# Outputs as 2x2 and 4x2 pixel patches in a lattice of convolutions on one Trainium2 core

## The chip, the cores and the metric

The kernel runs on one core of a Trainium2 chip. The metric is the device time of one execution in microseconds.

## The reference, cut to what matters

The input x is 8 images of 16 channels of 64x64, fp32. Four blocks add to it in turn, each on a group-normalised copy:

```python
x = x + L0(gn(x))     # lattice: 4x4 cells, each a 3x3 convolution + bias + relu
x = x + L1(gn(x))     # 3x3 convolution, 16 to 16 channels, circular borders
x = x + L2(gn(x))     # KAN: 3x3 over silu(v) and 8 cubic B-splines of v (9 features)
x = x + L3(gn(x))     # 3x3 convolution with bias
```

A lattice cell takes one to three groups of 16 channels (from the left, from below, from above) and gives groups to the right, up and down. Only the last cell's right output is used, so cells need one to three outputs. A cell's kind is (inputs)(outputs): cell 0 is 12, 1 and 2 are 13, 3 is 12, 4, 7, 8 and 11 are 22, 5, 6, 9 and 10 are 33, 12 and 15 are 21, 13 and 14 are 31. `gn` takes mean and variance over pairs of channels of an image.

## The kernel before, in words

**Products.** Every convolution is done as matmuls of 512 columns in float32r, three products for each term: high part of the weights by high part of the data, high by low, low by high. `split_hi` (ACT, line 994) copies an input piece as its high part, `split_lo` (DVE, line 1197) subtracts to get the low part, and in some kinds a DVE copy (line 1203) lays a shifted or doubled version on partitions 64 to 127, so that two products share a matmul.

**Patches.** An output tile has row parity on its partitions: 16 channels x outputs x 2, 4 or 8 image rows. Columns are on the free axis, rows of 66 with a zero column on each side, so the three column shifts are three matmuls (`TERMS`, line 126).

**Lattice.** `STEPS` is 16 cells x 8 images; step s is one image of one cell. For each step SyncE (line 605) loads the inputs from `DIN` in HBM into one of `SLOTS_K` = 2 raw slots once the low parts of step s - 2 are done; ACT and DVE split into `SLOTS_F` = 3 pieces; TensorE (line 1441) runs the matmuls into a ring of four banks; ACT (line 1004) evacuates with bias and relu into one of `SLOTS_S` = 3 staging slots; POOL (line 726) stores each output group to the `DIN` of the cell that takes it, with one DMA per group. The load of step s waits for the stores of the same image one cell earlier. `input_loads` (line 177) gives one DMA per input group and one to four for its halo rows: 15 DMAs in a 33 cell, 10 in 22, 9 in 31, 6 in 21, 5 in 13 and 12. The rows outermost are 16 to 128 on both sides.

**Weights.** TensorE turns the taps of cell k + 2 during cell k (`turn`), POOL stores them (line 696) and spreads them into the banded matrix of the next cell, a few DMAs per step (line 704). KAN weights are summed on POOL in cell 5 and spread in cell 15.

**Stages after the lattice.** Circular convolution, KAN and last convolution run one after the other, eight images each (`block_step`, line 1466, and the KAN loop behind it). The halo rows of a tile are fetched from partition to partition by SyncE (`halo_block`, line 610, for the single convolutions; `feature_halo`, line 639, for KAN with two DMAs for each of nine features, i.e. 18 per image). In KAN, TensorE does 81 matmuls on an image's own features and then 27 on its halo rows; SyncE starts an image's halos only when the halo pass of the image before is over, as the halo tiles are single. Features (`basis_act`, and the DVE loop of `ROUNDS`) are made in two rounds per image:

```python
if b:
    sp.wait_ge(tile_used, used(b - 1, "halo"))
for g in range(KAN_SETS):
    sp.wait_ge(feat_lo, KAN_SETS * b + g + 1)
    for t in range(GROUP * g, GROUP * (g + 1)):
        feature_halo(t, halo_rows[g])
```

**Start.** SyncE and POOL load x with 64 DMAs of 32 KB; ACT's queue first brings eight small loads (two of them the single-row `OB_IN`) and then zeroes the border rows of all `DIN` tensors with 32 DMAs, taken as 16 channels x images x rows of 66 numbers.

Of the kernel before, what the change touches and what calls it, by code (L numbers as in the profile page):

```python
# [8 lines left out]
YI = 8  # L27
YB = 8
WD = 64
HT = 64  # L30
PW = WD + 2
PIX = YB * WD
B = 8
X_SPLIT = 5
OUT_SPLIT = 5
RING = 4
HALO = 2 * C
# [5 lines left out]
MAIN_TILES = NG * K3 * NG  # L43
TILES = MAIN_TILES + K3 * NG
FSLOTS = 8
# [3 lines left out]

CB_COLUMNS = 48  # L50
HALO_FEATS = 3
GROUP = 4
KAN_SETS = 2
ROUNDS = KAN_SETS * B

CHUNK = YB * PW
SLAB = CHUNK + 2 * PW
PIECE = 4 * CHUNK
KSLOT = 8 * CHUNK
# [3 lines left out]
SLOTS_O = 4  # L63

RIGHT, UP, DOWN = range(3)
GN_EPS = 1e-5


class Count:


    def __init__(self):
        self.base, self.n = 0, 0

    def next(self):
        self.n += 1
        return self.base + self.n

    def enter(self, base):
        self.base, self.n = base, 0  # L80


class Cell:


    def __init__(self, k, n_in, outs):
        self.k, self.n_in, self.outs = k, n_in, outs
        self.m = m = len(outs)
        self.ry = {3: 2, 2: 4, 1: 8}[m]
        self.nb = HT // self.ry  # L90
        self.rows = m * self.ry * C
        self.plane_rows = self.ry * C
        self.nq = YI // self.ry
        self.run = self.nb * PW
        self.chunks = self.nb // YB
        self.kind = f"{n_in}{m}"
        self.pieces = 2 if self.kind == "33" else 1
        self.in_rows = 6 * C if self.kind == "12" else P
        self.dup_at = {"33": 2 * CHUNK, "13": 0, "22": 2 * CHUNK, "21": 2 * CHUNK}.get(self.kind)


def lattice():

    cells = []
    for col in range(4):
        for row in range(4):
# [9 lines left out]
            if row < 3:  # L116
# [4 lines left out]

TERMS = {"33": [(0, 0, 0), (0, 1, 1), (0, 2, 2), (2 * CHUNK, 0, 3), (2 * CHUNK, 2, 4)],
         "13": [(0, 0, 0), (0, 2, 1)],
         "12": [(0, 0, 0), (0, 1, 1), (0, 2, 2)],
         "22": [(0, 0, 0), (0, 1, 1), (0, 2, 2), (2 * CHUNK, 0, 3), (2 * CHUNK, 2, 4)],
         "21": [(g * CHUNK, dx, g * K3 + dx) for g in range(2) for dx in range(K3)]
               + [(2 * CHUNK, 0, 6), (2 * CHUNK, 2, 7)],
         "31": [(g * CHUNK, dx, g * K3 + dx) for g in range(3) for dx in range(K3)]
               + [(3 * CHUNK, dx, 9 + dx) for dx in range(K3)]}
TILES_OF = {"33": 5, "13": 2, "12": 3, "22": 5, "21": 8, "31": 12}  # L130
SPLIT = {"33": 4 * CHUNK, "13": 4 * CHUNK, "12": 2 * CHUNK, "22": 4 * CHUNK, "21": 3 * CHUNK, "31": 4 * CHUNK}


W_AT = {5: 0, 9: 0, 6: 960, 10: 960, 0: 1920, 3: 1920, 1: 2688, 2: 3072,
        4: 3456, 8: 3456, 7: 4736, 11: 4736, 13: 6016, 14: 0, 12: 9216, 15: 9216}
WA_SIZE = 9216 + 2 * 8 * P
Z_AT, Z_SIZE = 6016, 3072


def kernel_rows(cell):  # L140

    ry = cell.ry
    k16 = C
    for g in range(cell.n_in):
        if cell.kind == "33" and g < 2 or cell.kind == "12":
            for r in range(ry):
                yield g, r, g * 4 * k16 + r * k16, 3, 0, 0, 3, 0
        elif cell.kind in ("33", "13"):
            tile = 3 if cell.kind == "33" else 0
            for r in range(ry):  # L150
                yield g, r, r * k16, 3, 0, 0, 1, tile
                yield g, r, 4 * k16 + r * k16, 3, 0, 1, 1, tile
                yield g, r, r * k16, 3, 0, 2, 1, tile + 1
        else:
            base, tile = (g * 4 * k16, 0) if cell.kind == "22" else (0, g * K3)
            for r in range(ry):
                first, last = max(r - 1, 0), min(r + 1, ry - 1)
                yield g, r, base + first * k16, last - first + 1, first - r + 1, 0, 3, tile
            for side, r, ky in ((0, 0, 0), (1, ry - 1, 2)):
                row = g * 2 * k16 + side * k16  # L160
                if cell.kind == "31":
                    yield g, r, row, 1, ky, 0, 3, 9
                else:
                    tile_b = 3 if cell.kind == "22" else 6
                    yield g, r, row, 1, ky, 0, 1, tile_b
                    yield g, r, 4 * k16 + row, 1, ky, 1, 1, tile_b
                    yield g, r, row, 1, ky, 2, 1, tile_b + 1


def banded_rows():  # L170

    for r in range(YI):
        first, last = max(r - 1, 0), min(r + 1, YI - 1)
        yield r, first * C, last - first + 1, first - r + 1


def input_loads(cell):

    ry, nq = cell.ry, cell.nq

    def halos(g, top, bottom, col):
        if nq > 1:
            yield top, C, col + CHUNK, nq - 1, g, ry - 1, 0, 0
        yield top, C, col, 1, g, YI - 1, 0, -1
        if nq > 1:
            yield bottom, C, col, nq - 1, g, 0, 1, 0
        yield bottom, C, col + (nq - 1) * CHUNK, 1, g, 0, 0, 1

    if cell.kind in ("33", "13", "12"):
        for g in range(cell.n_in):  # L190
            row, col = (0, cell.run) if g == 2 else (g * 4 * C, 0)
            yield row + C, ry * C, col, nq, g, 0, 0, 0
            yield from halos(g, row, row + C + ry * C, col)
    else:
        own = 1 if cell.kind == "22" else cell.n_in
        for g in range(cell.n_in):
            if cell.kind == "22":
                yield g * 4 * C, ry * C, 0, nq, g, 0, 0, 0
            else:
                yield 0, P, g * CHUNK, 1, g, 0, 0, 0  # L200
        for g in range(cell.n_in):
            yield from halos(g, g * 2 * C, g * 2 * C + C, own * cell.run)


def build(nc, x, l0w, l0b, l1w, l2base, l2spline, l2scale, l2bias, l3w, l3bias, consts, out):
# [7 lines left out]
    pieces_before, chunks_before = [0], [0]  # L213
    stores_before = [1]
    loads_before = [[0], [0]]
    loads_of = []
    for cell in cells:
        loads_of.append(len(list(input_loads(cell))))
        n_stores = sum(1 for _, to, _ in cell.outs if to is not None)
        stores_before.append(stores_before[-1] + n_stores)  # L220
# [3 lines left out]
    for s in range(STEPS):  # L224
        loads_before[s % SLOTS_K].append(loads_before[s % SLOTS_K][-1] + loads_of[s // B])
    TOTP, TOTCH = pieces_before[-1], chunks_before[-1]
    dups_before = [0]
    for cell in cells:
        for b in range(B * cell.pieces):
            dups_before.append(dups_before[-1] + (cell.dup_at is not None))  # L230
# [1349 lines left out]
```

## Time and profile before

| | us |
|---|---|
| median of 3 runs (lowest, highest) | 1571.28 (1570.34, 1573.9) |
| profiled execution, own time | 1571.25 |
| its span, first to last instruction | 1569.4 |
| PE busy | 1408.7 |
| DVE, ACT, POOL busy | 818.7, 733.4, 706.0 |

Busy times of different engines overlap. PE's time is that of matmuls, which are pipelined. A window row gives what each engine was busy within a stretch of the span, the mean granted TensorE clock as a share of 2.4 GHz, and the mean share of time that the 16 DMA engines were busy. The stretches used are the stages: 0 to 62.4 us is before the first lattice matmul, 62.4 to 262.6 cells 0 to 3, to 329.3 cell 4, to 562.6 cells 5 and 6, to 687.2 cells 7 and 8, to 920.6 cells 9 and 10, to 980.5 cell 11, to 1030.3 cell 12, to 1172.1 cells 13 and 14, to 1299.0 cell 15, the circular convolution and the filling of the first features, to 1515.7 KAN, and the rest the last convolution.

### The profile page before, as it was taken

Reading aid. Unit: us, or ns where it says so; the run is one execution under the profiler, and the core shown is the slowest. Engines: PE = TensorE matmul, PEld = TensorE weight load, DVE = VectorE, ACT = ScalarE, POOL = GpSimd, SP = SyncE. Lnnn points to the kernel's source line nnn. Section 1 sums busy time; section 2 is a strip of 40 time slices with the busy share of each in tenths; the row PEclk is TensorE's granted clock in tenths of the full one; section 3 lists DMA queues with packets and bytes.
Section 4 is the critical chain, followed back from the end, with each engine's and each line's share of the span. In section 5 each row is a group of like instructions: output and inputs, shape, how many; then the busy total and the mean of one; then the engine's idle time right before and its main releaser. Section 6 shows DMA issues by size and latency. Waiting matters only on the chain.

```text
span 1569.4 us, 17219 instructions
## 1 busy us (share of the span) xinstructions
PE 1408.7 (90%) x6048; PEld 1038.1 (66%) x6048; DVE 818.7 (52%) x704; ACT 733.4 (47%) x745; POOL 706.0 (45%) x1132
## 2 busy tenths in 40 slices
PE   0498898989999999989999999999999538999997
PEld 0365566756666677766666677777777427777775
DVE  5346643545545535545555444423237479898832
ACT  0356654434444444444444434332233569788621
POOL 4344687745743445422323458965646510121212
PEclk9999999999999999999999999999999778999988
DMA  6577778797777677798777767665544202222123
GB/s 120 145 194 192 191 199 212 188 197 173 181 185 156 148 181 188 192 180 181 180 163 168 170 155 186 173 186 141 157 123 108 48 8 42 41 36 43 31 42 52
DMA packets 153530, 221.85 MB, mean 141 GB/s; under 512 B 64612, under 2 KB 77252, under 8 KB 153444
## 3 DMA queue, kind: packets, MB, share of 16 engines
q1 hardware_dynamic: 97472, 134.53, 37.7%
q0 software_dynamic: 46208, 83.65, 20.3%
q10 hardware_dynamic: 9764, 2.57, 1.1%
q8 instruction: 48, 0.79, 0.2%
q14 instruction: 38, 0.31, 0.1%
HBM read 130.52 MB, written 79.46 MB: 134 GB/s over the span
## 4 chain that ended last, share of the span: by engine, by line
PE 73%; DVE 9%; POOL 4%; issue 3%; ACT 3%; DMA 3%; SPq 2%; ACTq 2%; DVEq 0%; POOLq 0%
PE PB L1441 60%; PE PB L1414 11%; POOL WA L712 2%; DMA S<-lattice_in 2%; DVE S L1326 2%; DVE F L1197 2%; SPq L605 1%; ACT F L994 1%; PE PB L1398 1%; DVE F L1203 1%; ACTq L1015 1%; POOL WA L704 1%; DVE F L1308 1%; ACTq L1014 1%; SPq L624 1%
## 5 line engine op out<-in xcount | busy, mean ns | idle before, releaser
L1441 PE MATMUL PB<-F,WA 128*96 128x512 f32 (+2 forms) x4512 | 1099.3, 405 | 52.7 <-DVE F L1203 21.5
L1441 PEld LDWEIGHTS PB<-F,WA 128*96 128x96 f32 (+2 forms) x4512 | 792.0, 176 | 350.4 <-issue 56.0
L1197 DVE TENSOR_TENSOR F<-S,F 128x2112 fp32r<-128x2112 f32 (+2 forms) x160 | 352.3, 2202 | 561.2 <-ACT F L994 561.1
L1004 ACT ACTIVATE S<-PB,BIAS 96x512 f32<-96x512 f32 (+1 forms) x320 | 218.9, 686 | 607.8 <-PE PB L1441 607.7
L726 POOL DMA_DIRECT2D lattice_in<-S x264 | 155.7, 595 | 523.9 <-ACT S L1004 509.8
L704 POOL DMA_DIRECT2D WA<-taps_cell x512 | 310.6, 614 | 10.6 <-issue 5.9
L994 ACT ACTIVATE F<-S 128x2112 fp32r<-128x2112 f32 (+2 forms) x160 | 292.0, 1825 | 39.5 <-DMA S<-lattice_in 39.3
L1414 PE MATMUL PB<-F,WA 128*128 128x512 f32 (+1 forms) x864 | 210.7, 404 | 33.7 <-DVE F L1308 33.7
L1414 PEld LDWEIGHTS PB<-F,WA 128*128 128x128 f32 (+1 forms) x864 | 163.1, 190 | 78.1 <-issue 35.8
L1203 DVE CAST F<-F 64x2110 fp32r<-64x2110 f32 (+2 forms) x128 | 172.0, 1344 | 4.5
L685 POOL TENSOR_TENSOR RS<-VE,NHALF 128x1 f32<-128x1 f32 (+1 forms) x25 | 30.9, 1235 | 260.5 <-DVE VE L1163 260.4
L1414 PE MATMUL PB<-F,W 128*128 128x512 f32 (+1 forms) x240 | 69.0, 442 | 12.3 <-DVE F L1243 11.1
L1414 PEld LDWEIGHTS PB<-F,W 128*128 128x128 f32 (+1 forms) x240 | 48.0, 208 | 30.2 <-issue 16.6
L696 POOL DMA_DIRECT2D taps_cell<-WT x68 | 39.3, 588 | 16.1 <-DVE WT L1110 15.8
L938 ACT ACTIVATE S<-S 128x2112 f32<-128x2112 f32 x16 | 31.5, 1968 | 22.4 <-DVE S L1317 22.4
L908 ACT ACTIVATE S<-KS,CB 128x528 f32<-128x528 f32 x64 | 41.8, 724 | 0.3
L1110 DVE TENSOR_TENSOR WT<-PB,WT 48x432 fp32r<-48x432 f32 (+6 forms) x19 | 8.7, 455 | 59.1 <-ACT WT L978 59.1
L1319 DVE TENSOR_TENSOR S<-S 128x2112 f32<-128x2112 f32 x16 | 37.6, 2352 | 2.5 <-ACT S L918 2.5
L1308 DVE TENSOR_TENSOR F<-S,F 128x2112 fp32r<-128x2112 f32 x16 | 37.6, 2352 | 2.0 <-ACT F L927 2.0
L1326 DVE SCALAR_TENSOR_TENSOR S<-S 128x2112 f32<-128x2112 f32 x16 | 37.7, 2357 | 0.0
L1339 DVE TENSOR_TENSOR S<-S 128x2112 f32<-128x2112 f32 x16 | 37.6, 2351 | 0.0
L712 POOL DMA_DIRECT2D WA<-taps_kan x52 | 33.4, 649 | 5.3 <-issue 5.3
(106 smaller groups left out, 531.9 us busy)
## 6 DMA issues: line engine op xcount, KB each, us to landing
S<-lattice_in SPq DMA_DIRECT2D x272, 264.0 KB, 3.9
lattice_in<-S POOLq DMA_DIRECT2D x264, 264.0 KB, 4.3
S<-lattice_in SPq DMA_DIRECT2D x704, 33.0 KB, 3.6
S<-lattice_in SPq DMA_DIRECT2D x224, 99.0 KB, 4.7
F<-F SPq DMA_DIRECT2D x144, 57.8 KB, 2.2
WA<-taps_cell POOLq DMA_DIRECT2D x192, 9.0 KB, 3.3
lattice_in<-KS POOLq DMA_DIRECT2D x8, 264.0 KB, 3.4
S<-S SPq DMA_DIRECT2D x48, 32.9 KB, 2.0
```

The costliest lines, as they stand in the source:

```text
L704: pool.dma_start(dst, src).then_inc(w_loaded[k % 2], 16)
L712: pool.dma_start(dst, src).then_inc(loaded, 16)
L726: pool.dma_start(dst, src).then_inc(image_stored[b], 16)
L908: last = act.activation(UA[n % 2][:, j * TS:(j + 1) * TS], NS[b % 2], ACT.Abs, scale=2.5, bias=CB[:, t:t + 1])
L994: act.activation(piece_view(s, h, 0), raw_view(s)[h], ACT.Copy).then_inc(hi_ready, 1)
L1004: act.activation(to[:, c * YB:(c + 1) * YB, 1:WD + 1], RING_BANK[n % SLOTS_O][0:cell.rows, :].rearrange("p (y x) -> p y x", x=WD), ACT.Rel ...
L1197: last = nc.vector.tensor_tensor(piece_view(s, h, 1), raw_view(s)[h], piece_view(s, h, 0).bitcast(F32), ALU.subtract)
L1203: last = nc.vector.tensor_copy(FP[4 * C:P, piece_slot(i), :, first:end - 1], FP[0:4 * C, piece_slot(i), :, first + 1:end])
L1308: nc.vector.tensor_tensor(FQ[:, GROUP * g:GROUP * (g + 1), 1], U2[n % 2].rearrange("p (j f) -> p j f", j=GROUP), FQ[:, GROUP * g:GROUP * ( ...
L1326: nc.vector.scalar_tensor_tensor(w2, w2, 4.0, w, ALU.mult, ALU.mult).then_inc(kan_w3, 1)
L1414: last = nc.tensor.matmul(bank[:, :].rearrange("p (y x) -> p y x", x=WD), weights[0:rows, wp, tile, :], moving[:, :, dx:dx + WD], start=op ...
L1441: last = nc.tensor.matmul(bank, weights[0:rows, wp, tile, :], moving[:, :, dx:dx + WD], start=j == 0, stop=j == len(todo) - 1)
```

## The change

Column parity joins row parity on the partitions. A tile is 16 rows of 33 numbers (32 pixels of one parity and a zero); even and odd columns lie in two segments (`SEG`) of a row of the new HBM tensor `LAT`, with a zero between them, so stores and loads move whole runs. Outputs of a 33 or 13 cell are 96 partitions (3 groups x 2 rows), each column parity on its own; of a two-output cell 128 partitions of 2x2 patches; of a one-output cell, of KAN and of the single convolutions 4x2 patches. A term now covers two column shifts at once where columns are on partitions. Matmuls per image, which follow from the lists below: 33 56, 13 20, 12 12, 22 24, 21 18, 31 27, KAN 84 (54 own, 30 halo), single convolutions 12 each.

```diff
+RQ = 16
+RX = 32
+RW = RX + 1
+TS = RQ * RW
+EVEN = (RQ + 1) * RW
+PATCH = EVEN + TS
+SEG = 1 + EVEN + TS
+LEAD = 1 + TS
...
+    if kind in ("22", "21", "31"):
+        n = 2 if kind == "22" else 3
+        for dy in range(n):
+            for dx in range(2):
+                at, tile = ROW_AT[h + dy] + dx, ((1 - dx) * 2 + 1 - dy) if n == 2 else ((2 - dy) * 2 + 1 - dx)
+                todo += [(0, at, P, tile * P), (1, at, P, tile * P), (0, at, P, (2 * n + tile) * P)]
...
+COPIES = {"33": [(1, 2 * LEAD, 2 * LEAD, 2 * LEAD), (0, 2 * LEAD + 1, 3 * LEAD, LEAD - 1), (0, 3 * LEAD, 2 * LEAD, LEAD)],
+          "13": [(1, 0, 0, 2 * SEG), (0, 1, SEG, SEG - 1), (0, SEG, 0, SEG)],
+          "12": [(1, 0, 0, PATCH), (0, 1, 0, PATCH - 1)],
+          "31": [(1, PATCH, PATCH, PATCH), (0, PATCH + 1, PATCH, PATCH - 1)],
+          "22": [], "21": []}
...
+    LAT = nc.dram_tensor("lattice", (n_slots, B, HALO, 2 * SEG), F32, kind="Internal").ap()
```

The loads: in a 33 cell two DMAs that each take two input groups (slots `at` and `at + 1`), one for the third group, and 12 halo DMAs; in 22, 21 and 31 cells six DMAs of two groups, and in 31 six more of one group; in 12 six of one group.

```diff
+            if cell.m == 3:
+                n = min(cell.n_in, 2)
+                if cell.kind == "33":
+                    for row in range(2):
+                        yield KR[(1 + row) * HALO:(2 + row) * HALO, q, 0:2 * SEG], LAT[at:at + 2, b, row * C:(row + 1) * C]
+                    for g in range(2):
+                        yield from row_halos(KR[g * C:(g + 1) * C, q, 0:2 * SEG],
+                                             KR[3 * HALO + g * C:3 * HALO + (g + 1) * C, q, 0:2 * SEG], at + g, b)
+                last, col = (at + 2, 2 * SEG) if cell.kind == "33" else (at, 0)
+                yield KR[C:3 * C, q, col:col + 2 * SEG], LAT[last, b]
+                yield from row_halos(KR[0:C, q, col:col + 2 * SEG], KR[3 * C:4 * C, q, col:col + 2 * SEG], last, b)
+            else:
+                tiles = [(at, min(cell.n_in, 2), 0)] + ([(at + 2, 1, PATCH)] if cell.n_in == 3 else [])
+                for first, n, col in tiles:
+                    for r in range(2):
+                        for s in range(2):
+                            rows = slice((2 * r + s) * n * C, (2 * r + s + 1) * n * C)
+                            src = LAT[first:first + n, b, r * C:(r + 1) * C, s * SEG:(s + 1) * SEG] if n > 1 \
+                                else LAT[first, b, r * C:(r + 1) * C, s * SEG:(s + 1) * SEG]
+                            if r == 0:
+                                yield KR[rows, q, col:col + PATCH], src[..., 1 - s:1 - s + PATCH]
+                            else:
+                                yield KR[rows, q, col:col + EVEN], src[..., LEAD - s:LEAD - s + EVEN]
+                                yield KR[rows, q, col + EVEN:col + PATCH], src[..., 1 - s:1 - s + TS]
```

The stores: three DMAs in a three-output cell, four of two groups each in a two-output cell, four in a one-output cell and for each normalised input image.

```diff
+            if cell.m == 3:
+                for o in range(3):
+                    yield LAT[to[o], b], st[o * HALO:(o + 1) * HALO, 0:2 * SEG]
+            elif cell.m == 2:
+                for r in range(2):
+                    for s2 in range(2):
+                        rows = (2 * r + s2) * HALO
+                        yield (LAT[to[0]:to[1] + 1:to[1] - to[0], b, r * C:(r + 1) * C, s2 * SEG:(s2 + 1) * SEG],
+                               st[rows:rows + HALO, 0:SEG])
```

The zero fills of ACT's queue are gone: the zeros come with the staged tiles. x is loaded with 32 DMAs of 64 KB into `XROW` and its columns are parted by 8 ACT and 8 DVE copies. The output is brought back to whole rows in `OT` and stored with four DMAs per image.

The circular convolution of image j runs in step j + 3 of cell 15. DVE's order there is the lattice update, the update of circular image b - 4, statistics and the low part of circular image b - 2; SyncE puts eight halo DMAs per image behind the loads of step b:

```diff
+                if k == NC - 1 and b >= 4:
+                    l1_halos(b - 4)
+            for j in range(4, B):
+                l1_halos(j)
...
+            for b in range(B):
+                if b:
+                    sp.wait_ge(tile_used, used(b - 1, "halo"))
+                for g in range(KAN_SETS):
+                    sp.wait_ge(feat_lo, KAN_SETS * b + g + 1)
+                    for t in range(GROUP * g, GROUP * (g + 1)):
+                        feature_halo(t, halo_rows[g])
+                    if g == 0:
+                        sp.wait_ge(silu_lo, b + 1)
+                        feature_halo(BASES, halo_rows[KAN_SETS])
+                if b >= 3:
+                    l3_halos(b - 3)
```

`feature_halo` now has four DMAs per feature (two sides x two column parities), 36 per image, and `l3_halos` four. The last convolution of image b - 3 stands in KAN's image b:

```diff
+            for b in range(B):
...
+                if b == B - 1:
+                    group_means(2, B - 2)
+                if b >= 3:
+                    l3_step(b - 3)
+                for g in range(KAN_SETS):
+                    pe.wait_ge(halo_rows[g], (b + 1) * 64 * GROUP)
+                    for t in range(2 * g, 2 * g + 2):
+                        halo_step(bank, t, False)
+                pe.wait_ge(halo_rows[KAN_SETS], (b + 1) * 64)
+                halo_step(bank, PAIRS - 1, True).then_inc(tile_used, 1)
+            l3_step(B - 3)
+            group_means(2, B - 1)
+            l3_step(B - 2)
+            l3_step(B - 1)
```

`l3_step(b)` waits for `l3_lo` and for the four DMAs of `l3_halos(b)` (`pe.wait_ge(l3_halo[z], ...)`).

## Rows read from the trace of the kernel before

**Rows 1.** The page: busy time of PE, and the costliest group of instructions.
```profile
PE 1408.7 (90%) x6048; PEld 1038.1 (66%) x6048; DVE 818.7 (52%) x704; ACT 733.4 (47%) x745; POOL 706.0 (45%) x1132
...
L1441 PE MATMUL PB<-F,WA 128*96 128x512 f32 (+2 forms) x4512 | 1099.3, 405 | 52.7 <-DVE F L1203 21.5
```

**Rows 2.** Windows by stage: us, PE, PEld, DVE, ACT, POOL busy (instructions), clock, DMA share, GB/s.
```profile
0.00:62.40 62.40, 4.47 (x42) 3.91 (x43) 30.49 (x62) 9.78 (x13) 26.90 (x53) 1.00 0.61 128
62.40:262.60 200.20, 176.80 (x780) 124.92 (x781) 100.44 (x55) 113.30 (x135) 119.04 (x198) 0.96 0.75 195
262.60:329.30 66.70, 60.97 (x258) 47.73 (x259) 29.79 (x18) 28.19 (x26) 37.72 (x62) 0.96 0.83 193
329.30:562.60 233.30, 233.28 (x995) 158.13 (x996) 118.25 (x66) 101.67 (x96) 114.14 (x167) 0.99 0.76 171
562.60:687.20 124.60, 119.46 (x519) 93.62 (x518) 59.38 (x35) 55.55 (x52) 65.90 (x107) 0.99 0.76 191
...
920.60:980.50 59.90, 59.90 (x262) 47.12 (x261) 28.19 (x17) 25.70 (x25) 51.48 (x81) 1.00 0.71 180
980.50:1030.30 49.80, 48.08 (x211) 37.55 (x209) 20.42 (x16) 18.52 (x19) 43.72 (x77) 1.00 0.63 179
1030.30:1172.10 141.80, 141.75 (x648) 111.91 (x649) 38.79 (x19) 40.31 (x33) 80.41 (x141) 1.00 0.52 152
1172.10:1299.00 126.90, 76.95 (x323) 60.28 (x321) 84.78 (x178) 65.42 (x100) 55.41 (x96) 0.83 0.24 53
1299.00:1515.70 216.70, 210.46 (x878) 165.34 (x879) 175.76 (x146) 164.65 (x141) 26.97 (x14) 0.99 0.23 41
1515.70:1569.40 53.70, 43.17 (x147) 29.39 (x145) 16.29 (x29) 8.73 (x13) 14.20 (x26) 0.81 0.25 44
```

**Rows 3.** The DMA view: a queue's packets; issues by tile, KB each, us to landing.
```profile
q10 hardware_dynamic: 9764, 2.57, 1.1%
...
F<-F SPq DMA_DIRECT2D x144, 57.8 KB, 2.2
...
lattice_in<-WA ACTq DMA_DIRECT2D x12, 99.0 KB, 5.2
...
lattice_in<-WA ACTq DMA_DIRECT2D x12, 66.0 KB, 4.3
...
lattice_in<-WA ACTq DMA_DIRECT2D x8, 33.0 KB, 3.3
...
RAW<-in_L_conv_W ACTq DMA_DIRECT2D x2, 81.0 KB, 3.0
...
G<-in_consts ACTq DMA_DIRECT2D x1, 64.0 KB
...
CB<-in_consts ACTq DMA_DIRECT2D x1, 24.0 KB
IDF<-in_consts ACTq DMA_DIRECT2D x1, 9.0 KB
BN_IN<-in_L_conv_b ACTq DMA_DIRECT2D x1, 3.0 KB
OB_IN<-in_L_conv_bias_weight ACTq DMA_DIRECT2D x1, 0.1 KB
OB_IN<-in_L_conv_bias ACTq DMA_DIRECT2D x1, 0.1 KB
```

**Rows 4.** Windows again: a stretch in which the DMA engines are fully busy.
```profile
136.80:138.40 1.60, 1.60 (x8) 1.06 (x7) 1.56 (x2) 0.85 (x2) 0.10 (x1) 1.00 1.02 363
```

**Rows 5.** Timeline of the KAN stage, matrix engine and SyncE's halo DMAs: start, duration, instruction.
```profile
1346.06 17.41 PE L1414 MATMUL PB<-F,WA 96*128 96x512 f32 x72
...
1357.86 0.59 SPq L643 DMA_DIRECT2D F<-F  x1
1358.49 0.60 SPq L644 DMA_DIRECT2D F<-F  x1
...
1364.52 0.59 SPq L643 DMA_DIRECT2D F<-F  x1
```

More of the change, by code:

```diff
@@ L50 @@
 CB_COLUMNS = 48
-HALO_FEATS = 3
 GROUP = 4
@@ L130 @@
[L130 to L167, printed above, removed]
@@ L170, in banded_rows @@
[L170 to L202, printed above, removed]
+ROW_AT = (0, EVEN, RW)
@@ new lines, in output_stores @@
+        def output_stores(s):
+            k, b = divmod(s, B)
+            cell, st = cells[k], staged(s)
+            to = [slot_of[target, g] for _, target, g in cell.outs if target is not None]
+            if cell.m == 3:
[7 more added lines that the diff above has]
+                               st[rows:rows + HALO, 0:SEG])
+            else:
+                yield from image_store(to[0], b, st)
@@ new lines, in image_store @@
+        def image_store(slot, b, st):
+            for s in range(2):
+                for h in range(2):
+                    rows = s * 4 * C + h * HALO
+                    if h == 0:
+                        yield LAT[slot, b, :, s * SEG:s * SEG + TOP], st[rows:rows + HALO, 0:TOP]
+                    else:
+                        yield LAT[slot, b, :, s * SEG + TOP:(s + 1) * SEG], st[rows:rows + HALO, 1:1 + TS]
+        loads_before = [[0], [0]]
+        for s in range(STEPS):
+            loads_before[s % SLOTS_K].append(loads_before[s % SLOTS_K][-1] + len(list(input_loads(s))))
@@ L539, in build @@
                 w_after[cell.k] = n
+        W2_DMAS = sum(dma_total(kan_spread(what)) for what in range(3))
         PER = 4
@@ L1192, in split_lo @@
+            dve.wait_ge(dve_step, next(steps))
+            nc.vector.tensor_copy(EDGE_HI[:, :], f).then_inc(dve_step, 1)
+            dve.wait_ge(dve_step, next(steps))
+            nc.vector.tensor_tensor(cube, f, EDGE_HI[:, :].bitcast(F32), ALU.subtract).then_inc(edge_ready, 1)
             def split_lo(s):
-                for h in range(cells[s // B].pieces):
+                cell = cells[s // B]
+                for h in range(cell.pieces):
+                    slot = (pieces_before[s] + h) % SLOTS_F
@@ L1437, in cell_step @@
-                        for j, (at, dx, tile, wp, fp) in enumerate(todo):
-                            rows = 6 * C if cell.kind == "12" or cell.kind == "31" and tile >= 9 else P
-                            moving = FP[0:rows, piece_slot(i), fp, at + c * TS:at + (c + 1) * TS]
-                            moving = moving.rearrange("p (y w) -> p y w", w=PW)
-                            last = nc.tensor.matmul(bank, weights[0:rows, wp, tile, :], moving[:, :, dx:dx + WD],
+                        bank = pixels(RING_BANK[n % SLOTS_O][0:cell.rows, :])
@@ L1442, in cell_step @@
+                        h, parity = (c, 0) if cell.m < 3 else divmod(c, 2)
+                        todo = terms(cell.kind, h, parity)
+                        for j, (part, at, rows, tile) in enumerate(todo):
+                            first = W_AT[k] + tile
+                            last = nc.tensor.matmul(bank, WA[0:rows, first:first + cell.rows],
+                                                    wide(FP[0:rows, i % SLOTS_F, part, at:at + TS])[:, :, 0:RX],
                                                     start=j == 0, stop=j == len(todo) - 1)
```

1454 lines of the change are left out of this document (793 added, 661 removed).

## The prediction, made before the changed kernel ran

> **What bounds the kernel now.** First the page's sums: the matrix engine is busy 1408.7 of 1569.4 us, the four others about half or less, and line 1441 (the lattice) alone holds 1099.3 us in 4512 matmuls [rows 1]: 244 ns each. The other matmul line, 1414, runs the three single convolutions. Then the windows by stage [rows 2]: in cells 5 and 6 PE is busy 233.28 of 233.3 us, in cells 13 and 14 141.75 of 141.8; in cells 0 to 3 it is idle for 23.4 of 200.2 us; between the start of cell 15 and the first KAN matmul it is busy 77.0 of 126.9 us; in the KAN stage 210.5 of 216.7. So PE sets the pace of most of the lattice and of KAN, and the loads with their split do in cells 0 to 3. The DMA share stands at 0.71 to 0.83 through cells 4 to 11: high, though nothing waits there yet.
>
> **Matmuls removed.** Per image, old against new: a 33 cell 60/56, 13: 24/20, 12: 18/12, 22: 30/24, 21: 24/18, 31: 36/27, KAN 108/84, circular 12/12, last convolution 18/12. Over 16 cells and 8 images this is 5616 against 4656, 960 fewer, and at 244 ns 234 us. It all counts only where PE stays the bound. From the stage windows [rows 2] PE alone would give: cells 5, 6, 9, 10 a step of 14.3 -> 13.4 us (cells 9 and 10 took as long as 5 and 6), 22 cells (4, 7, 8, 11: 66.7 + 124.6 + 59.9 = 251.2 us, 7.3 to 8.3 a step) -> 5.8, cells 13 and 14 8.9 -> 6.6.
>
> **The loads, which decide.** The new input_loads fetches two input groups with one DMA: `LAT[first:first + 2, b, rows]` is 2 x 16 rows in memory, against 32 partitions. The old loads have 16 to 128 rows outermost on both sides. Is the work of such a DMA spread over all 16 DMA engines? ACT's queue q10 tells [rows 3]. Its zero fills move 264-byte rows: 12 x 99 + 12 x 66 + 8 x 33 KB = 8704 packets. The other eight have 48 (IDF), 2 x 48 (RAW), 48 (BN_IN), 128 (CB), 128 (G) and 2 x 1 rows (OB_IN): 450. The queue counts 9764, so 610 are left over; 38 DMAs x 16 + 2 x 1 is 610. I read these as one closing packet per engine that takes part: a DMA with 16 or more rows outermost runs on 16 engines, the two of a single row on one each. BN_IN's rows are also 64 bytes and it gets 16, so the outermost count decides and not the size. For an outermost count of 2 on one side and 32 on the other the ends are 2 engines and 16. I take 2: both sides must be handed out alike, and a side that has only two outermost steps can be cut only in two. Whether it is always the same two no row shows: with rotating pairs the load would even out and cost what 16 engines cost, with a fixed pair all of it piles up. I take the fixed pair for SP's loads (a queue that keeps nothing from one DMA to the next has no reason to move) and leave rotation with the first rival; for POOL's stores of this form I take a sixteenth per engine.
> The Trainium skill's page "DMA: Bandwidth & Descriptors", section "Why a DMA increments its semaphore by 16 and not by 1", says the engine count is the largest up to 16 that divides the slowest dimension of both sides, and that queues of SP take the lowest-numbered ones. It agrees with the leftover of 610, and by it every one of these loads would meet on the same two engines.
> A fully busy stretch moved 363 GB/s, 22.7 per engine; cell 4 as a whole only 193 / (0.83 x 16) = 14.5, with waiting inside the packets [rows 2, 4]. Two engines with work queued are nearest to the first: 22.7.
> Per step, on the two engines:
> - 22: four blocks of 32 x 1089 x 4 bytes = 558 KB, 279 KB per engine, 12.3 us; its four stores (558 KB) go from the POOL queue, a sixteenth per engine, 1.5. Sum 13.8 against 5.8 of PE. With two input slots a next load is always queued, so the step is 13.8: 32 steps 442, plus 6 for two entries into 33 cells, against 251.2: **+197**.
> - 33: two blocks of 32 x 2180 x 4 bytes, again 279 KB per engine, 12.3; the rest of the loads (1091 KB) and the stores (837 KB), spread over 16: 3.0 + 2.3. Sum 17.6 against 13.4 of PE: 563 against 466.7 (233.3 twice): **+96**.
> - 31: 12.3 + 0.8 (third group) + 0.8 (stores) + 0.2 (weights) = 14.1; 16 steps 226 against 141.8: **+84**.
> - cell 12: 13.3 a step, 106 against 49.8: **+57**.
> - cell 15: 12.5 a step.
> Cells of one input (0 to 3) have no such block. PE gives up 160 of 672 matmuls there, 39 us at most, but two images' worth of load, ACT split and DVE subtraction must fit in two steps, and the new split adds copies. Between -39 and +15 I take 0.
> PE will be idle in these steps and run part of the time at 1.2 GHz (windows with a granted clock under 1 stand before KAN, at 0.83 [rows 2]); 24 matmuls of 512 columns at 427 ns each are 10.2 us, still under 13.8, so it costs nothing there.
>
> **Start.** 32 zero fills vanish from the front of the DMA engines (DMA share 0.61 in the first 62.4 us [rows 2]) and the image loads are half as many; splitting columns and four stores per image instead of one cost some back. Bounds 0 and -25: **-12**.
>
> **Circular convolution into cell 15.** An image's chain is now: split (DVE), 8 halo DMAs at 0.64 us on SP [rows 5] and 2.2 to land [rows 3], 12 matmuls, and in the next step the two updates on DVE (2.4 us each). Per two steps that is 5.1 + 2.2 + 2.9 + 4.4 + 0.7 + 6.3 = 21.6, 11 a step, and the halos also stand behind the load on SP and on its two engines: 15. Cell 15: 3 x 12.5 + 5 x 15 = 113; three images' drain 28; filling the features 22 (one hat group is done early). 163 against 126.9: **+36**. With 16 engines the same chain gives 91 + 22 = 113, **-14**.
>
> **KAN and the last convolution.** KAN looks like the gain (24 matmuls, 5.9 us per image) and the last stage (45 of 53.7 us) is to hide in it. But SP now issues 36 halo DMAs per image, not 18, each 0.64 us apart (1357.86 to 1358.49), starting only when the halo pass of the image before is over (1346.06 + 17.41 = 1363.47, first issue 1364.52: 1.05 us) [rows 5]. So 1.05 + 36 x 0.64 + 2.2 landing + 18 matmuls (4.4) = 30.7 per image, already over today's 27.4. From image 3 on, l3_step(b - 3) stands on PE ahead of all halo passes and waits for l3_halos, which SP issues behind image b's 36: 1.05 + 40 x 0.64 + 2.0 + 42 matmuls (10.2) + 2 for the slow clock after some 15 us of idleness = 40.5. DVE (about 25 us of work per image, 2.2 more now) lies inside. 3 x 31.5 + 5 x 40.5 + a tail of 26 (last halo pass, statistics, rows, halos, 12 matmuls, stores) = 323 against 216.7 + 53.7 = 270.4: **+52**.
>
> **Sum** against the profiled execution's own 1571.25 us (span 1569.4; the median of the runs is 1571.28, the same): 197 + 96 + 84 + 57 + 36 + 52 + 0 - 12 = +510. Forecast **2080 us**.
>
> **Rivals.**
> *All 16 engines carry the two-group blocks, at once or in rotation.* For: every DMA of 16 rows and more does so today, and no row shows an outermost 2. Then the loads are lighter than today (a 22 step 558 KB, half of today's) and PE stays the bound: 22 cells -39, 33 -31, 31 -25 (a step of 7.1, by the load of 12 DMAs with its split and copies), cell 12 -5 (POOL's issues), start -12, cells 0 to 3 +5, cell 15 -14, KAN +52: 1571 - 69 = **1502**. This is the faster side; its price is the engine count, and it decides from about 6 engines up, where the 22 load falls under 6 us.
> *PE sets everything*, KAN too: 1571 - 234 = **1337**. Against: SP's 36 issues alone are 23 us of a 20.5 us image.
> *The two engines run at the loaded rate*, 14.5 GB/s: 19.2 us per block set, a 22 step 21.6, a 33 step 27.5: about +250 and +320 on their own, in all near **2750**. Against: there is little else on those two.
>
> **Numbers.** Two engines 0.80 (2080); 16 engines 0.14 (1502); PE alone 0.02; loaded rate 0.04. Between 22.7 GB/s and a fifth less or a little more, and with -39 to +15 and 0 to -25 above, the first case spans 1850 to 2400, and as it holds 8 in 10 this is the range. A measurement of this kernel tells 0.2% from no change. Faster 0.16, same 0.01, slower 0.83.
>
> **What would show it.** Right: in the 22 cells PE busy about 5.8 of 13.8 us, a step of 17 to 18 us in the 33 cells, landing of the SP loads over 10 us, a mean DMA share that falls while the loads are late, ACT's split waiting for the load; in KAN a 15 us idle PE before the last convolution's matmuls. Wrong: PE solid through cells 4 to 14, or the count of closing packets in SP's queue still 16 per load.

## The result, and the profile after

The changed kernel takes 2211.24 us (median of 4 runs, 2203.45 to 2218.42) against 1570.81 us for the kernel before (4 runs, 1567.8 to 1573.9): a ratio of 1.4076, 95% interval 1.402 to 1.4132. It is slower by 41%. The forecast was 2080, with a range of 1850 to 2400. The profiled execution has a span of 2211.3 us.

The page of the changed kernel: busy time by engine, then three of its costliest groups (busy, mean ns of one, idle before and what ended it).

```profile
PE 1454.5 (66%) x5088; PEld 982.0 (44%) x5088; DVE 792.0 (36%) x952; ACT 697.5 (32%) x740; POOL 631.2 (29%) x1018
...
L1559 PE MATMUL PB<-F,WA 128*128 128x512 f32 (+2 forms) x3792 | 1157.1, 463 | 554.5 <-issue 305.2
...
L1037 ACT ACTIVATE F<-S 128x2116 fp32r<-128x2116 f32 (+4 forms) x160 | 261.4, 1635 | 1171.6 <-DMA S<-lattice 1171.6
L937 POOL DMA_DIRECT2D lattice<-S x432 | 244.7, 575 | 1141.4 <-ACT S L1048 1138.0
```

Set beside [rows 1], PE issues 960 matmuls fewer and is busy for longer: 305 ns a matmul in the lattice (1157.1 / 3792), against 244 before (1099.3 / 4512). Part of them ran at 1.2 GHz: the granted clock is 0.74 to 0.88 in the lattice rows below, and was 0.96 to 1.00 in [rows 2]. ACT's split of the inputs (line 1037) waits 1171.6 us for the loads.

The windows by stage, which answer to [rows 2]: cells 0 to 3, cell 4, cells 5 and 6, cells 7 and 8, then cell 12, cells 13 and 14, cell 15 to KAN, and KAN to the end. The bounds are the first matmul of a stage: 56.3 cell 0, 313.1 cell 4, 428.4 cell 5, 746.9 cell 7, 962.5 cell 9, 1272.3 cell 11, 1375.9 cell 12, 1480.7 cell 13, 1705.0 cell 15, 1883.3 KAN.

```profile
56.30:313.10 256.80, 180.17 (x585) 102.53 (x585) 125.45 (x114) 111.14 (x131) 107.82 (x167) 0.81 0.59 150
313.10:428.40 115.30, 63.16 (x210) 48.02 (x211) 13.71 (x14) 21.25 (x26) 30.00 (x49) 0.74 0.39 107
428.40:746.90 318.50, 257.28 (x951) 155.19 (x951) 127.12 (x159) 96.39 (x97) 89.39 (x154) 0.88 0.52 129
746.90:962.50 215.60, 124.57 (x422) 94.57 (x421) 24.70 (x23) 40.58 (x52) 58.12 (x93) 0.75 0.36 104
...
1375.90:1480.70 104.80, 53.59 (x162) 40.37 (x163) 13.12 (x12) 14.56 (x17) 43.82 (x74) 0.74 0.34 97
1480.70:1705.00 224.30, 137.99 (x451) 104.86 (x451) 64.55 (x62) 41.35 (x33) 68.61 (x104) 0.74 0.32 91
1705.00:1883.30 178.30, 87.91 (x273) 63.97 (x273) 86.25 (x163) 78.81 (x92) 73.53 (x98) 0.68 0.18 41
1883.30:2211.30 328.00, 227.66 (x784) 167.03 (x784) 174.73 (x164) 162.37 (x147) 23.04 (x46) 0.81 0.40 69
```

In cells 7 and 8 the matrix engine is busy 124.6 of 215.6 us with a mean DMA share of 0.36. Before, it was 119.5 of 124.6 us with 0.76. So the engines as a whole are idle while the loads are late. That is what a load that uses only a few of them looks like.

The chain that ended last, in cells 7 and 8 (start, length, what): one piece for each second step, each a wait of 17 to 20 us for a load.

```profile
747.24 18.53 DMA S<-lattice
...
773.34 17.92 DMA S<-lattice
...
799.07 19.61 DMA S<-lattice
...
827.68 17.28 DMA S<-lattice
```

The DMA queues (packets, MB, share of 16 engines) and the halo DMAs of KAN:

```profile
q1 hardware_dynamic: 70560, 131.33, 24.0%
q0 software_dynamic: 78528, 99.75, 18.7%
...
q10 hardware_dynamic: 548, 0.27, 0.1%
...
F<-F SPq DMA_DIRECT2D x232, 61.9 KB, 2.3
```

Against [rows 3], q10 has lost 9216 packets (9764 - 548), the 32 zero fills with 8704 rows and 32 x 16 closing packets; a halo DMA still lands in 2.3 us, and there are twice as many of them per image.

Where the time went, stage by stage, in the profiled executions (us; bounds as above, each kernel's own first matmuls). "Split" and "best" are both_split and all_edge of the experiments.

| stage | before | forecast | after | split | best |
|---|---|---|---|---|---|
| start | 62.4 | 50.4 | 56.3 | 57.7 | 58.1 |
| cells 0 to 3 | 200.2 | 200.2 | 256.8 | 218.5 | 211.5 |
| 22: cells 4, 7, 8, 11 | 251.2 | 448 | 434.6 | 215.5 | 212.6 |
| 33: cells 5, 6, 9, 10 | 466.7 | 563 | 628.3 | 481.7 | 440.1 |
| cell 12 | 49.8 | 106 | 104.8 | 50.9 | 47.8 |
| 31: cells 13, 14 | 141.8 | 226 | 224.3 | 138.4 | 117.7 |
| cell 15, circular, first features | 126.9 | 163 | 178.3 | 149.8 | 122.6 |
| KAN and last convolution | 270.4 | 323 | 328.0 | 331.2 | 273.3 |

### The profile page after: what moved, and what is told of

It reads as the page before. It is cut to its first block, busy times and chain, and to the rows that moved or that the text cites. A ratio compares the mean times of both kernels' runs of the same rounds, so it can differ in the third digit from the quotient of the medians.

```text
span 2211.3 us, 15351 instructions
## 1 busy us (share of the span) xinstructions
PE 1454.5 (66%) x5088; PEld 982.0 (44%) x5088; DVE 792.0 (36%) x952; ACT 697.5 (32%) x740; POOL 631.2 (29%) x1018
## 4 chain that ended last, share of the span: by engine, by line
DMA 38%; SPq 23%; PE 15%; DVE 12%; issue 4%; ACT 4%; POOL 3%; ACTq 0%; DVEq 0%; POOLq 0%
DMA S<-lattice 36%; SPq L696 20%; PE PB L1531 8%; PE PB L1559 6%; ACT F L1037 4%; DVE F L1337 4%; SPq L710 3%; DVE F L1327 2%; DVE F L1329 2%; DVE F L1330 2%; POOL F L969 1%; DVE S L1440 1%; DVE F L1418 1%; DVE F L1333 0%; DVE F L1334 0%
## 5 line engine op out<-in xcount | busy, mean ns | idle before, releaser
L1559 PE MATMUL PB<-F,WA 128*128 128x512 f32 (+2 forms) x3792 | 1157.1, 463 | 554.5 <-issue 305.2
L1559 PEld LDWEIGHTS PB<-F,WA 128*128 128x128 f32 (+2 forms) x3792 | 758.3, 207 | 946.5 <-issue 583.1
L1037 ACT ACTIVATE F<-S 128x2116 fp32r<-128x2116 f32 (+4 forms) x160 | 261.4, 1635 | 1171.6 <-DMA S<-lattice 1171.6
L937 POOL DMA_DIRECT2D lattice<-S x432 | 244.7, 575 | 1141.4 <-ACT S L1048 1138.0
L1327 DVE TENSOR_TENSOR F<-S,F 128x1089 fp32r<-128x1089 f32 (+2 forms) x80 | 121.5, 1518 | 650.0 <-ACT F L1037 649.9
L1531 PE MATMUL PB<-F,WA 128*128 128x512 f32 x576 | 164.1, 447 | 88.2 <-POOL KAN L974 42.0
L1329 DVE TENSOR_TENSOR F<-S,F 128x1058 fp32r<-128x1058 f32 x64 | 80.7, 1261 | 392.6 <-ACT F L1037 391.6
L1337 DVE CAST F<-F 64x1058 fp32r<-64x1058 f32 (+6 forms) x304 | 193.3, 685 | 1.5
L1531 PEld LDWEIGHTS PB<-F,WA 128*128 128x128 f32 x576 | 121.6, 216 | 127.5 <-issue 78.5
L1330 DVE TENSOR_TENSOR F<-S,F 64x1058 fp32r<-64x1058 f32 x64 | 79.8, 1246 | 0.0
```

Of the source, the lines that this page charges most:

```text
L937: pool.dma_start(dst, src).then_inc(image_stored[b], 16)
L1037: act.activation(piece_view(s, h, 0), raw_view(s, h), ACT.Copy).then_inc(hi_ready, 1)
L1327: last = nc.vector.tensor_tensor(lo, raw, hi, ALU.subtract)
L1329: nc.vector.tensor_tensor(lo[:, 0:2], raw[:, 0:2], hi[:, 0:2], ALU.subtract)
L1330: last = nc.vector.tensor_tensor(lo[0:4 * C, 2:4], raw[0:4 * C, 2:4], hi[0:4 * C, 2:4], ALU.subtract)
L1337: last = nc.vector.tensor_copy(FP[4 * C:P, slot, part, to:to + n], FP[0:4 * C, slot, 0, source:source + n])
```

## The experiments

**1. both_split: one DMA per group.** Loads and stores of two groups go through a generator that splits them; layout and bytes stay.

```diff
+def by_group(pairs):
+    for out, src in pairs:
+        if len(out.shape) == 3 and out.shape[0] == 2 and len(src.shape) == 2:
+            for g in range(2):
+                yield out[g], src[g * C:(g + 1) * C]
+        elif len(src.shape) == 3 and src.shape[0] == 2 and len(out.shape) == 2:
+            for g in range(2):
+                yield out[g * C:(g + 1) * C], src[g]
+        else:
+            yield out, src
...
-                for dst, src in input_loads(s):
+                for dst, src in by_group(input_loads(s)):
...
-                    for dst, src in output_stores(s):
+                    for dst, src in by_group(output_stores(s)):
```

> Every load and store of two groups is issued as two DMAs of one group (16 rows outermost on both sides); the bytes and the layout stay. If the blocks of two groups run on 2 engines each (my theory), the loads get light and the next bound per step is SyncE's issuing, 0.63 us a DMA: 22 and 21 cells 12 x 0.63 = 7.6, about 8 us a step (now 13.6 and 13.1), 33 cells 17 x 0.63 = 10.7 under PE's 13.4, about 14 (now 19.6), 31 cells 18 x 0.63 = 11.4 (now 14.0), cells 0 and 3 back to 5.5 (now 7.9), cell 15 -25: in all -180 -180 -40 -41 -35 -25, about 1710 us. SyncE's queue would show 16 closing packets for every DMA: 18656 + 448 x 30 = 32096 packets of 4 bytes. If the engine count isn't the cause, 448 more issues can only cost: 2211 us or more.

Measured: 1641.77 us (4 runs), ratio to before 1.0446 (1.041 to 1.0481): 569 us of the 640 come back, with 640 more DMAs issued. Its SyncE queue:

```profile
q1 hardware_dynamic: 84000, 131.38, 40.2%
```

That is 13440 packets more than in the changed kernel for the same data rows, and 13440 = 448 x 30: each of the 448 two-group loads had left 2 closing packets and is now two DMAs with 16 each. Counted alone, the 4-byte packets are 18656 in the changed kernel and 32096 here, as expected. The steps came out better than I expected in three kinds (22: 6.7 us, 21: 6.4, 31: 8.6); SyncE issues their simpler loads every 0.46 us, not every 0.63. The 33 cells came out worse (15.1), although PE is busy there all the time. Experiment 5 takes that up.

**2. loads_split: only the loads**, with the stores left in pairs.

> Only the loads of two groups are split by group; the stores of two groups in the 12 and 22 cells stay. My theory: 33, 31, 21 cells as with both split (14, 11.4, 8 us a step); 22 cells about 9, as a store of 139 KB still takes an engine pair 5.4 us; cells 0 and 3 stay at about 7.9. About 1780 us. If the stores are what matters, close to 2211.

Measured: 1781.77 us (ratio 1.1328, 1.1295 to 1.136). The loads alone are worth 429 us. 33 cells 480.8 us and 31 cells 141.6, as with both split; cells 0 to 3 stay at 251.1; the 22 cells take 309.4, or 9.7 us a step.

**3. stores_split: only the stores.**

> Only the stores of two groups (12 and 22 cells) are split by group. My theory: the loads still meet on one engine pair, so 33, 31 and 21 cells stay; 22 cells 13.6 -> 12.3 us a step (-40), cells 0 and 3 7.9 -> 5.5 (-35): about 2135 us. If the stores were the heavier part, below 1950.

Measured: 2163.71 us (ratio 1.3764, 1.3734 to 1.3793), 48 us won: 31 in cells 0 to 3 (225.5) and only 11 in the 22 cells (423.9), where I had expected 40, while 33, 31 and 12 did not move. The two together are worth more than their sum (569 against 429 + 48): with the loads already split, splitting the stores too brings the 22 cells from 309.4 to 215.5, 94 us. So the stores' cost there stands behind that of the loads until the loads are quick. The POOL queue of this kernel:

```profile
q0 software_dynamic: 38592, 99.59, 19.5%
```

39936 packets fewer, though 192 more DMAs: a two-group store leaves 240 packets of 4 bytes, two of one group 32 (192 x 208 = 39936).

**4. l3late: the last convolution behind the halo passes.**

```diff
-                if b >= 3:
-                    l3_step(b - 3)
                 for g in range(KAN_SETS):
...
                 halo_step(bank, PAIRS - 1, True).then_inc(tile_used, 1)
+                if b >= 3:
+                    l3_step(b - 3)
```

> In an image of KAN the last convolution of image b - 3 is put behind the halo passes instead of ahead of them; nothing else moves. My theory (it waits for the four halo DMAs that SyncE issues last, and with it all halo passes wait, and so the next image's halos): images 3 to 7 take 31 us as images 0 to 2 do, not 42.5: -50, about 2160 us. Rival: DVE's feature work, or the statistics behind it, set the 42.5 us; then less than 15 us is won.

Measured: 2201.23 us; KAN and last convolution 328.2 us against 328.0. The expected gain is absent, so the edit did not remove the bound; the 10 us between the medians are not in this stage. The timeline of DVE in l3late shows where the wait went:

```profile
2043.83 1.52 DVE L1409 SCALAR_TENSOR_TENSOR OT<-PB,OB,X 64x512 f32<-64x512 f32 x2 [15.95 <-PE PB L1531]
2045.38 2.36 DVE L1440 SCALAR_TENSOR_TENSOR S<-S 128x2112 f32<-128x2112 f32 x1
2047.65 2.35 DVE L1418 TENSOR_TENSOR F<-S,F 128x2112 fp32r<-128x2112 f32 x1
```

The update of the last convolution (line 1409) stands in DVE's order ahead of the features of the next image (line 1418), for which SyncE's first halos wait. Late on PE, it holds DVE for 15.95 us. Either way the period of an image holds SyncE's 36 issues, then the four halos behind them, then the last convolution. The order on SyncE is the cause, and PE's place only chooses who waits.

**5. wide_rows: no change of the row count inside a bank** (on both_split).

```diff
-        todo.append((0, shifted(rest, s, 2), 4 * C, first + 384))
+        todo.append((0, shifted(rest, s, 2), P, first + 384))
...
+            for k, at in ((1, 384), (2, 384), (5, 960), (6, 960)):
+                last = nc.vector.memset(WA[4 * C:P, W_AT[k] + at:W_AT[k] + at + 96].bitcast(F32), 0.0)
```

> On both_split (1641.8). In the 33 and 13 cells one matmul of every bank uses 64 rows, the others 128; its weights are now 128 rows, the lower half zero, so nothing else changes. With both split a bank of 14 matmuls in a 33 cell starts its matmuls 238 ns apart, but 326, 398 and 317 ns apart around the one of 64 rows. Theory: the change of the row count costs these 327 ns a bank, 1.3 us in a step of four banks: 33 cells 15.1 -> 13.8 us a step (-42), 13 cells 8.1 -> 7.3 (-13), about 1587 us. Rival: the gap comes from something else at that place (the shifted operand, the bank's change); then it stays at about 1642.

Measured: 1591.42 us (ratio 1.0133, 1.0107 to 1.0159), 50 us less, of them 39 in the 33 cells: 442.8 us (13.8 a step). The 13 cells take 7.35 and 7.0. Timeline of PE in 33 cells (5 and 6), of both_split and then of wide_rows:

```profile
427.04 28.24 PE L1572 MATMUL PB<-F,WA 128*96 128x512 f32 x108
```

```profile
405.50 49.85 PE L1577 MATMUL PB<-F,WA 128*96 128x512 f32 x209 [1.54 <-ACT F L1051]
```

28.24 / 108 is 261 ns a matmul, 49.85 / 209 is 239 ns. Both are fully busy stretches, and the columns are the same. Over a bank, here the group of 14 matmuls that are added up in one place, the 22 to 23 ns are some 0.32 us: a single 64-row matmul among 128-row ones costs that on top of its own 0.24 us.

**6. l3first: SyncE issues the last convolution's halos early** (on both_split).

```diff
                 for g in range(KAN_SETS):
+                    if g == 1 and b >= 3:
+                        l3_halos(b - 3)
                     sp.wait_ge(feat_lo, KAN_SETS * b + g + 1)
...
-                if b >= 3:
-                    l3_halos(b - 3)
```

> On both_split (1641.8, KAN and last convolution 331). SyncE issues the four halo DMAs of the last convolution of image b - 3 between the silu feature's and the second group's, not behind all 36. Putting the last convolution late on PE won 10 us only, since DVE waits for its result ahead of the features of the next image: it is a wait for l3_halos either way. Theory: with these halos early, nobody waits for them, and images 3 to 7 take 31 us as images 0 to 2, not 42.5: -50, about 1592 us. Rival: DVE's or ACT's own work sets the 42.5: within 15 us of 1642.

Measured: 1591.06 us (ratio 1.0131, 1.0106 to 1.0155), 51 us less, of them 46 in KAN and the last convolution (331.2 to 285.1). The starts of the halo pass of three images in its timeline are 34 us apart (31 were expected, 42.5 stood before):

```profile
1420.86 3.20 PE L1544 MATMUL PB<-WX,WA 128*128 128x512 f32 x12
...
1454.70 4.61 PE L1544 MATMUL PB<-WX,WA 128*128 128x512 f32 x12
...
1488.88 3.22 PE L1544 MATMUL PB<-WX,WA 128*128 128x512 f32 x12
```

**7. l3first_pool: 12 of the 36 issues moved to POOL.** A function like `feature_halo` stands in POOL's program (silu, and features 6 and 7), with a semaphore of its own.

> l3first, and 12 of the 36 feature halo DMAs of an image (silu, and two features of the second group) are issued by POOL instead of SyncE. If SyncE's issuing (0.63 us each) still bounds the image at 31 us, it falls to 1.05 + 28 x 0.63 + 2.3 landing + about 4 = 25, and DVE's or PE's 26 to 28 us bound it: another -25, about 1565 us. Rival: DVE bounds it already at 30 to 31 us: no more than 5 us.

Measured: 1578.57 us (7 runs; ratio 1.0059, 1.0039 to 1.0078), 12 us less, 15 in this stage (270.1): neither the 25 I expected nor the rival's 5 at most. The period falls to about 32 us:

```profile
1403.29 3.23 PE L1566 MATMUL PB<-WX,WA 128*128 128x512 f32 x12
...
1434.51 3.23 PE L1566 MATMUL PB<-WX,WA 128*128 128x512 f32 x12
...
1467.01 3.23 PE L1566 MATMUL PB<-WX,WA 128*128 128x512 f32 x12
```

So issuing did bound it, but only by some 2 us an image. What sets the 32 us now was not separated.

**8. paired: another layout, same number of loads** (on the changed kernel). The first two groups of a cell lie as image, row parity, group, channel, so a load of two groups reads one run of 32 rows; stores into such a pair are cut to 16 rows.

```diff
+            view = LAT[at:at + 2].rearrange("g b h f -> (g b h) f").rearrange(
+                "(b r n) f -> b r n f", b=B, r=2)
+            pair_of[at], pair_of[at + 1] = (view, 0), (view, 1)
...
-                    yield KR[(1 + row) * HALO:(2 + row) * HALO, q, 0:2 * SEG], LAT[at:at + 2, b, row * C:(row + 1) * C]
+                    yield KR[(1 + row) * HALO:(2 + row) * HALO, q, 0:2 * SEG], pair_rows(at, b, row)
```

> On the changed kernel (2211). The two input groups of a cell lie as one run of 32 rows in HBM, so that a load of two groups stays one DMA but has 32 rows outermost on both sides; stores into such a pair are issued per row parity with 16 rows. Engine theory: as both_split, with half the issues on SyncE: 22 cells 6.7 -> 6.3 us a step, 31 8.65 -> 7.2, 21 6.4 -> 5.7, cell 15 -15, about 1580 us; closing packets in SyncE's queue 16 for each of its 1558 DMAs (24928). If the loads were slow because one DMA holds two groups, and not by the outermost count, it stays near 2211.

Measured: 1609.05 us (ratio 1.0245, 1.022 to 1.027). One DMA still brings two groups to 32 partitions, so holding two groups was not what was slow. Its SyncE queue:

```profile
q1 hardware_dynamic: 76832, 131.35, 36.0%
```

6272 packets more than in the changed kernel, 448 x 14: the same DMAs close on 16 engines instead of 2. The 31 cells gained most against both_split (138.4 to 117.3), as they had had 18 issues a step. The 22 cells and cell 15 gained less than expected (2 us, not 13, and 5, not 15), most of what is missing to 1580.

**9. paired_all: paired, wide_rows and l3first_pool together.**

> paired (1609.1), wide_rows and l3first_pool together. If the three act in different stages and their savings add up: 1609 - 50 (33 and 13 cells) - 56 (KAN and last convolution 326 -> 270) = 1503 us, faster than the kernel before by 4%. Rival: PE no longer covers something in the lattice and part comes back as waits on the loads: 1520 to 1550.

Measured: 1495.8 us, ratio to before 0.9521 (0.9499 to 0.9543). The savings add up.

**10. all_edge: the constant halo rows from DVE** (on paired_all). The first KAN matmul waits for POOL (timelines of the changed kernel, POOL and PE):

```profile
1844.96 2.31 POOL L969 CAST F<-EDGE 64x33 fp32r<-64x33 f32 x1
1847.34 0.58 POOL L969 CAST F<-EDGE_HI 64x33 fp32r<-64x33 f32 x1
1847.98 2.22 POOL L969 CAST F<-EDGE 64x33 fp32r<-64x33 f32 x1
...
1883.28 2.04 PE L1531 MATMUL PB<-F,WA 128*128 128x512 f32 x4 [42.01 <-POOL KAN L974]
```

```diff
-                            pool.tensor_copy(tile[rows, part, side * (RQ - 1)], const).then_inc(edge_step, 1)
...
-                            pool.wait_ge(edge_step, n)
...
+                            last = nc.vector.tensor_copy(tile[rows, part, side * (RQ - 1)], const)
```

> On paired_all. The 32 constant rows of KAN's halo tiles are written by DVE instead of POOL, which takes 0.2 to 2.4 us for each (38 us in all) while DVE works, and for whose end the first KAN matmul and the first halo DMA wait (42 us idle PE). As 32 copies of some 0.16 us they are 5 us on DVE. Theory: the first KAN matmul comes some 20 us earlier, as the features are ready then: -20, about 1483 us. Rival: the features of the first image are what PE waits for anyway, and DVE's 5 us are added: +5.

Measured: 1483.87 us (6 runs, 1476.53 to 1488.75), ratio to before 0.9433 (0.9409 to 0.9457), 12 us less than paired_all. The two copies of a row pair now take 0.27 us on DVE, and what ends the idle time before KAN is the features:

```profile
1191.45 0.27 DVE L1440 CAST F<-EDGE_HI 64x33 fp32r<-64x33 f32 x2
...
1210.34 10.01 PE L1588 MATMUL PB<-F,WA 128*128 128x512 f32 x30 [20.85 <-DVE F L1475]
```

The stage from cell 15 to KAN is 22.9 us shorter (145.5 to 122.6) in the profiled executions; other stages, which the edit does not touch, were some 12 us longer in all (cells 0 to 3 by 5.1, the start by 3.4), and I leave that open. This version beats both kernels.

## Why the prediction was right, and where it was off

**The sum as a whole.** The forecast was 131 us short of the measured time: 66 us of that are in the 33 cells, 57 in cells 0 to 3 and 15 in the stage from cell 15 on, while the 22 cells came out 14 us shorter than forecast. The mechanism was right; the two large misses are terms of the sum, named below.

**Matmuls removed: the count was right, the price not quite.** With all fixes the 22 cells take 212.6 us against 251.2 (-39), 31 -24, 33 -27. The terms of the rival with 16 engines were -39, -25 and -31. For the 22 cells that is not PE's work alone: 5.8 us a step would have been -66, and in cell 4 of both_split PE is busy 50.64 of 59.0 us. The rival's -39 stood without its working, so its match is luck. In the changed kernel itself a 33 cell's matmuls are not 244 ns: experiment 5 shows 261, 1.3 us a step, which no row of before could show: in its cell 5 the matmuls start some 240 ns apart throughout.

**The loads: right, and most of the loss hangs on it.** Splitting loads and stores brings back 569 of the 640 us. The sign does not hang on it alone: both_split is still 4.5% slower than the kernel before, and paired 2.5%. The step "a side that has only two outermost steps can be cut only in two", taken from the 610 closing packets of [rows 3], is confirmed by count (2 per DMA, 16 with another layout) and by time (experiments 1, 2 and 8). The fixed pair fits as well: 22 cells came to 13.6 us a step against 13.8, 31 to 14.0 against 14.1, cell 12 to 13.1 against 13.3. With pairs that rotate and work side by side these loads would have cost about what they cost in both_split. The DMA view of the changed kernel from 760 to 830 us, in cells 7 and 8 (GB/s in 40 slices, and SyncE's queue), shows the pair itself:

```profile
GB/s 129 48 49 51 52 78 157 181 111 50 50 94 83 128 203 94 48 49 52 49 134 158 195 159 134 63 47 99 156 142 110 48 48 53 52 74 119 202 157 82
...
q1 hardware_dynamic: 1180, 3.08, 11.3%
```

Between the bursts of the stores the core moves 48 to 53 GB/s, about 25 for each of two engines, and two of 16 engines are 12.5%. Counted from the start and length of each packet (the 4-byte ones left out), SyncE's queue has exactly two packets in flight for 9.3 to 10.1 us of a step in the 22, 33 and 31 cells and in cell 12, though several loads stand queued; in cells 7 and 8 of both_split it is 0.4 us. So the queued loads never ran on different pairs at the same time. That it is the same pair from one load to the next fits this, but the profile does not name the engine of a packet.
By the Trainium skill's "DMA: Bandwidth & Descriptors", section "Why a DMA increments its semaphore by 16 and not by 1", the engines of such a load are the lowest-numbered two. The count of two agrees with the 18656 closing packets; which two they are no run shows.

That the steps met the sum within 0.2 us is partly luck. The sum for a 22 cell was 12.3 us for the loads and 1.5 for the stores, but at 25 GB/s the loads are 11.2, and in experiment 3 the stores' form was worth 0.3 us a step. What makes up the rest was not separated. PE was busy for 7.8 of 13.5 us a step in cells 7 and 8, not 5.8 of 13.8, at a granted clock of 0.75.

**The 33 cells: the mechanism right, one term short.** Forecast 17.6 us a step (+96), measured 19.6 (+162). Of the 2 us, 1.3 are the row-count gap only if PE were on the path, which it is not there (busy 257 of 318 us). The sum gave the other traffic, 3.0 + 2.3 us, the unloaded rate of a sixteenth each. The 22 cells, where the sum held, have the same load on the pair and no further loads beside it, so I suspect the 3.0 + 2.3 us. The packets bear this out: in cells 5 and 6 SyncE's queue has two packets in flight for 9.5 us of a step of 19.9, as in the 22 cells, but more than two for 7.5 us, against 1.3 in cells 7 and 8. So the blocks themselves hardly got dearer; the time beside them is about 10 us (4 in cells 7 and 8) where the sum had 5.3 (and 1.5). Whether the engines or SyncE's 15 issues in a row set it stays open.

**Cells 0 to 3: the term that failed.** The text said "cells of one input have no such block" and took 0, between -39 and +15; measured +57. The loads have none, but the stores of cells 0 and 3 are of the two-group form. The sum gave such stores "a sixteenth per engine", as a mean over a rotation. That the stores' form costs time here is shown: the changed kernel's cells 0 and 3 took 7.6 and 8.1 us a step, and with stores_split 5.5 and 6.3, 31 of the 57 us. How it does is my reading and not shown: a single store stands on few engines, and the loads on these wait with it. Cells 1 and 2 are 15 us of the 57. Part of that may be the 64-row matmul: wide_rows brings them from 8.0 and 8.1 us a step to 7.35 and 7.0, about what they were before. But l3first, which keeps the 64-row matmul, took 7.45 and 7.7, and all_edge, which does not have it, 7.8 and 7.3, so these runs do not show how much.

**Start:** -6 against -12, within the bounds of 0 and -25.

**Cell 15 and the circular convolution:** +51 against +36. The step chain and its drain were about right (136 us against 141), and "filling the features 22" was the short one: PE waits 42 us for POOL's 32 constant copies, and with these on DVE the stage is 22.9 us shorter (experiment 10).

**KAN and the last convolution:** 328.0 us against 323. The period was forecast as 40.5 us and the timeline gives 42.4, and its parts are those of the sum. SyncE's first issue to the end of the four late ones (in the changed kernel):

```profile
2059.14 1.22 SPq L710 DMA_DIRECT2D F<-F  x2
...
2082.53 2.50 SPq L717 DMA_DIRECT2D WA<-WA  x4
...
2086.81 5.75 PE L1531 MATMUL PB<-WA,W 128*128 128x512 f32 x12 [5.72 <-issue]
...
2101.51 10.15 SPq L710 DMA_DIRECT2D F<-F  x16
```

2059.14 to 2085.03 are the 40 issues, 1.8 us later the last convolution starts, at 1.2 GHz (5.75 us for 12, which take 3.3 elsewhere in this stage), and at 2101.51 the next image's halos begin. One sign did not come: PE is not idle for 15 us before the last convolution, but for 5.79 and 5.72 us, with 24 of the next image's own matmuls in between. What the prediction left out is DVE's order: l3late showed that moving the wait on PE alone gives nothing. "DVE lies inside" holds for its work, not for its place in the chain. Moving the four issues on SyncE gave 46 us.

**The rivals.** "All 16 engines carry the blocks" is excluded by the closing packets, the two packets in flight and experiment 8. That paired_all came to 1495.8, near its 1502, is chance: a kernel whose blocks run on 16 engines takes 1609 by itself (paired), and 1495.8 only with KAN mended and the 64-row matmul taken out. So this rival missed by 107 us; it forgot the matmul gap and POOL's copies. "PE sets everything" (1337) is far off in every version. "Loaded rate" (2750) did not happen: the pair ran near the unloaded rate.

## What to carry to other kernels

Before merging two DMAs into one, read the outermost dimension on both sides: here a leading 2 put each load of SyncE's queue on two engines, and the loads queued behind it did not use others. The sign in the profile is a low mean DMA share beside long waits for loads; the closing packets of a queue give the count. Lay the data so that the merged dimension is one run, and store in pieces instead: that kept the number of loads and turned +41% into -5.7% together with four small mends.
When a wait moves on one engine and the time stays, look for the next engine that waits for the same result ahead of its main work.

## What the runs showed of the hardware that I had not expected

- One 64-row matmul among 128-row ones stretches a bank of 14 by 327 ns (start to start 326, 398 and 317 ns around it, 238 elsewhere); with 128 rows and zero weights all are some 238 apart. The Trainium skill's "TensorEngine Tiling (Array Packing)", section "Tiling Modes", says that changing the tiling mode drains the engine; it gives no time, and these 327 ns agree with such a drain. That a 64-row matmul among 128-row ones is such a change is my reading.
- A POOL copy of 64 x 33 numbers took 0.2 us when DVE stood still and up to 2.4 us when one of its long operations ran: in the changed kernel one from 1844.96 to 1847.27 us ended with DVE's operation from 1844.85 to 1847.21. The 32 in a row, each waiting for the one before, took 37 us.
- A POOL store whose outermost count is 2 leaves 240 packets of 4 bytes, every other POOL DMA leaves 16 (866 DMAs in the changed kernel: 674 x 16 + 192 x 240 = 56864; 1058 with stores_split: 1058 x 16 = 16928). What the 240 are I can't tell.
- SyncE issues a load of whole runs in 0.42 us (0.46 from start to start), a halo with two segments in 0.59 (0.63 from start to start, as in [rows 5]).
